# Layer 0 of a two-layer graph network: one-hot numbers read from PSUM, and GpSimd's gathers without waits for the one-hot rows

## What is computed

```python
h = jnp.maximum(_layernorm(x), 0.0)
msgs = h[src]                                            # layer 0
summed = segment_sum(msgs, dst, num_segments=num_dst)
h_neigh = summed / jnp.maximum(deg, 1.0)[:, None]
x = x + relu(h @ W_self + h_neigh @ W_neigh + b)
h = jnp.maximum(_layernorm(x), 0.0)
xs = h[src]                                              # layer 1
e = sigmoid(relu(concat([xs, h[dst]]) @ We1 + be1) @ We2 + be2)
m = e * xs
m_sum, m_max = segment_sum(m, dst), segment_max(m, dst)
x = x + relu(concat([m_max, m_sum, h]) @ Wn1 + bn1) @ Wn2 + bn2
```

## Time and profile before

| | us |
|---|---|
| median of 3 runs (5727.77 to 5729.11) | 5728.72 |
| span of the profiled execution | 5726.5 |
| GpSimd busy | 4144.7 (72%) |
| VectorE busy | 4244.9 (74%) |
| TensorE busy | 3700.0 (65%) |
| ScalarE busy | 1898.2 (33%) |

### The profile page before, as it was taken

The page is one execution under the profiler, slowest core; times in us unless marked ns, Lnnn a source line. Parts: engine busy times, 40 slices in busy tenths (PEclk is TensorE's granted clock), DMA queues, the critical chain, the costliest instruction groups (busy, mean ns, idle before and its releaser), DMA issues.

```text
span 5726.5 us, 110353 instructions
## 1 busy us (share of the span) xinstructions
PE 3700.0 (65%) x25175; PEld 3357.9 (59%) x25176; DVE 4244.9 (74%) x9019; ACT 1898.2 (33%) x4035; POOL 4144.7 (72%) x3884
## 2 busy tenths in 40 slices
PE   0001888988888888545566666666666667767771
PEld 0001878888888888545555555556555666666660
DVE  5788778877777777467777777777787778888881
ACT  6101777877777777401111111111111111111110
POOL 5243666888888888777777777777777777777766
PEclk9999999999999999855555555555555555555555
DMA  7210112434344443443333333333444434444440
GB/s 233 77 36 14 25 40 66 122 122 125 121 124 125 124 125 123 139 107 104 106 111 107 113 111 113 111 113 111 119 113 117 119 112 124 117 119 126 123 114 22
DMA packets 402218, 611.87 MB, mean 107 GB/s; under 512 B 191933, under 2 KB 274979, under 8 KB 402107
## 3 DMA queue, kind: packets, MB, share of 16 engines
q0 software_dynamic: 182688, 377.75, 24.2%
q1 hardware_dynamic: 150357, 130.12, 7.1%
q10 hardware_dynamic: 69094, 103.21, 5.9%
HBM read 470.99 MB, written 118.43 MB: 103 GB/s over the span
## 4 chain that ended last, share of the span: by engine, by line
POOL 45%; issue 21%; PE 12%; DVE 11%; DMA 3%; DVEq 2%; ACTq 2%; ACT 2%; POOLq 1%; SPq 0%; PEld 0%
POOL counts_f L572 23%; POOL extra_f L572 16%; PE ps_acc L1785 5%; POOL records L594 2%; PE ps_acc L1884 2%; DVE msg L1443 1%; POOL own_rows L618 1%; PE ps_acc L1815 1%; DMA counts_f<-hA_table,stage 1%; DVE act_w L1432 1%; PE ps L1807 1%; DVE chunk_max L1448 1%; POOL out_dram L717 1%; DVE pre L1037 1%; DVE hot L1270 1%
## 5 line engine op out<-in xcount | busy, mean ns | idle before, releaser
L572 POOL DMA_INDIRECT counts_f<-hA_table,stage x2496 | 2368.2, 949 | 783.4 <-issue 751.2
L1785 PE MATMUL ps_acc<-msg,ident 128*128 128x64 f32 (+1 forms) x4974 | 1229.8, 427 | 1013.6 <-DVE msg L1443 1013.6
L1785 PEld LDWEIGHTS ps_acc<-msg,ident 128*128 128x128 f32 x4974 | 1115.4, 328 | 1119.5 <-DVE msg L1443 1117.8
L1601 ACT ACTIVATE counts_f<-ps 128x784 bf16<-128x784 f32 x1568 | 1267.8, 823 | 427.2 <-PE ps L1807 363.8
L572 POOL DMA_INDIRECT extra_f<-hA_table,estage x780 | 1085.1, 1391 | 237.7 <-issue 232.3
L1815 PE MATMUL ps_acc<-pieces_f,counts_f 128*128 128x192 bf16 x9604 | 1035.1, 249 | 1.8 <-ACT counts_f L1601 1.2
L1807 PE MATMUL ps<-hot 128*128 128x196 bf16 x6272 | 829.8, 256 | 226.5 <-ACT counts_f L1601 153.6
L1693 ACT ACTIVATE ps<-z,be_col 128x4 f32<-128x4 f32 x854 | 228.2, 267 | 2214.4 <-DVE z L1438 1954.8
L1426 DVE TENSOR_TENSOR pre<-counts_f,ps 128x512 f32 (+1 forms) x854 | 585.4, 685 | 482.5 <-SPq L864 310.0
L1815 PEld LDWEIGHTS ps_acc<-pieces_f,counts_f 128*128 128x128 bf16 x9604 | 897.0, 139 | 3.3 <-issue 2.1
L1807 PEld LDWEIGHTS ps<-hot 128*128 128x128 bf16 x6272 | 545.0, 99 | 318.3 <-issue 292.3
(11 more groups left out here) (244 smaller groups left out, 3228.1 us busy)
## 6 DMA issues: line engine op xcount, KB each, us to landing
early_rows<-extra_f SPq DMA_DIRECT2D x196, 384.0 KB
counts_f<-early_rows ACTq DMA_DIRECT2D x98, 768.0 KB
counts_f<-hA_table,stage POOLq DMA_INDIRECT x2496
counts_f<-counts_f SPq DMA_DIRECT2D x78, 288.0 KB, 2.6
own<-own_rows ACTq DMA_DIRECT2D x98, 128.0 KB, 2.2
extra_f<-hA_table,estage POOLq DMA_INDIRECT x780
hA_table<-node ACTq DMA_DIRECT2D x98, 96.0 KB
sorted_rows<-srt SPq DMA_DIRECT2D x14, 252.0 KB, 2.6
```

The lines of the kernel that those rows point to most:

```text
L572: return pool.indirect_dma_start(to, None, table, bass.IndirectOffsetOnAxis(ap=idx, axis=axis))
L1601: act.activation(counts[:, c, nodes, :].rearrange("p (b h) t -> p b (h t)", h=2), ps_pairs[g & 1][:, :].rearrange("p (b w) -> p b w", b=BA ...
L1785: return pe.matmul(ps_sum[:, 0:D], ident[:, :], rows, start=False, stop=False, skip_group_check=True)
```

## The change

The numbers stay in PSUM. `load_edges` loads the lists of two tiles so that partition a holds nodes 2a and 2a + 1 side by side. Partitions 0 to 63 are then one tile and 64 to 127 the next, and `edge_ids` copies 128 columns once. A transpose of 64 partitions now gives even nodes on partitions 0 to 63 and odd ones on 64 to 127 at once. `edge_values` and `val` are gone; the one-hot instruction reads `ps_val` in `ps_t`. As that buffer is single, the transposes of the next tile's numbers wait until this tile's one-hots are all made (`s_hot`), and stand before the pairs of group 12. VectorE's first one-hots of a phase wait for them (`s_tr`). `edge_ids` moves to the second phase of a pair. The other transposes move from `ps_t` to `ps_y`; for that `cat_transpose` stands after group 7, `cat_copy` after eviction 8 and `product` after group 9. GpSimd's `spread` waits are removed.

```diff
-        idx_lo = sb("idx_lo", [P, 2, 2, RUN], BF16)
-        idx_hi = sb("idx_hi", [P, 2, 2, RUN], BF16)
-        val = sb("val", [P, 2, 2, PAIRS], BF16)
+        idx_lo = sb("idx_lo", [P, 2 * RUN], BF16)
+        idx_hi = sb("idx_hi", [P, 2 * RUN], BF16)
...
-        ps_idx = ps_t[:, 0:P].bitcast(BF16)
+        ps_val = ps_t[:, 0:PAIRS].bitcast(BF16).rearrange("p (w n) -> p w n", w=2)
+        ps_T = ps_y[:, 0:P]
+        ps_new = ps_y[:, P:P + D]
+        ps_ab = ps_y[:, BANK // 2:BANK]
...
-                        if spread and n % half == half // 2:
-                            wait_alone(pool, s_hot, jj * (8 * SUBS) + (c * (4 * SUBS) + (2 + n // half) * (2 * SUBS) + 6))
...
-            def load_edges(t, c):
-                sp.dma_start(win[:, c, :], sorted_rows[bass.ds(t * P, P), 0:RUN]).then_inc(s_win[c], 16)
+            rows_by_two = sorted_rows.rearrange("(a h) w -> a h w", h=2)
+            def load_edges(q):
+                sp.dma_start(win[:, :, :], rows_by_two[bass.ds(q * P, P), :, 0:RUN]).then_inc(s_win, 16)
...
-                v.tensor_copy(idx_lo[:, :, :, :], twice(src_lo[:, :])).then_inc(s_prep, 1)
-                v.tensor_copy(idx_hi[:, :, :, :], twice(src_hi[:, :])).then_inc(s_prep, 1)
+                v.tensor_copy(idx_lo[:, :], src_lo[:, :]).then_inc(s_prep, 1)
+                v.tensor_copy(idx_hi[:, :], src_hi[:, :]).then_inc(s_prep, 1)
...
-                    wait_alone(v, s_val, q * 4 + (2 * c + 2))
+                    wait_alone(v, s_tr, q * 2 + (c + 1))
...
-                    ids = val[:, c, which, s * SUB_PAIRS:(s + 1) * SUB_PAIRS].rearrange("p (b e) -> p b e", e=2)
+                    ids = ps_val[:, which, s * SUB_PAIRS:(s + 1) * SUB_PAIRS].rearrange("p (b e) -> p b e", e=2)
...
-                if ids and c == 0:
+                if ids and c == 1:
                     edge_ids(q + 1)
...
-            def edge_values(q, k):
...
-                    act.activation(val[half, k & 1, :, :], by_parity[half, :, :, h], ACT.Copy).then_inc(s_val, 1)
...
-                    if g == 4 and ids:
-                        edge_values(q, c + 1)
...
-                    if g == 7 and mean:
+                    if g == 8 and mean:
                         cat_copy(q - 1, c)
...
+                half = slice((k & 1) * PAIRS, ((k & 1) + 1) * PAIRS)
...
-                    last = pe.transpose(ps_idx[:, w * P:(w + 1) * P],
-                                        ids[:, k & 1, :, :].rearrange("p h k -> p (h k)"), ident_b[:, :])
+                    last = pe.transpose(ps_val[:, w, :], ids[half, :], ident_b[half, half])
...
+                    if g == 12 and ids:
+                        wait_alone(pe, s_hot, q * (4 * SUBS) + (c + 1) * (2 * SUBS))
+                        edge_transposes(q, c + 1)
...
-                    if g == 4 and ids:
-                        edge_transposes(q, c + 1)
-                    if g == 6 and mean:
-                        if ids:
-                            wait_alone(pe, s_val, q * 4 + (2 * c + 4))
+                    if g == 7 and mean:
                         cat_transpose(q - 1, c)
-                    if g == 8 and mean:
+                    if g == 9 and mean:
                         product(q - 1, c)
```

More of the change, by code:

```diff
@@ L425, in gnn_kernel @@
         s_xadd = sem("s_xadd")
-        s_win = [sem(f"s_win{c}") for c in range(2)]
+        s_win = sem("s_win")
         s_prep = sem("s_prep")
         s_tr = sem("s_tr")
-        s_val = sem("s_val")
         s_hot = sem("s_hot")
@@ L684, in _ @@
                     early_gather(jj, c, READY[1])
-            early_gather(TPAIRS // 2, 0, READY[1], spread=False)
+            early_gather(TPAIRS // 2, 0, READY[1])
             early_rest(GROUPS_L0)
@@ L785, in next_tiles @@
                     wait_alone(sp, s_prep, q * 2 + 2)
-                    for c in range(2):
-                        load_edges(q * 2 + (c + 2), c)
+                    load_edges(q + 1)
                 wait_alone(sp, s_x1, q * 2 - 2)
@@ L792, in _ @@
                 sp.wait_ge(s_srtw[h], 16 * TITER)
-            for t in range(2):
-                load_edges(t, t)
+            load_edges(0)
             sp.wait_ge(s_h0w, H0_DMAS)
@@ L798, in _ @@
             sp.wait_ge(s_prep, 2)
-            for t in range(2, 4):
-                load_edges(t, t & 1)
+            load_edges(1)
             sp.wait_ge(s_prep, 4)
-            for t in range(4, 6):
-                load_edges(t, t & 1)
+            load_edges(2)
             for q in range(2, 5):
@@ L1245, in edge_ids @@
             def edge_ids(q):
-                for c in range(2):
-                    v.wait_ge(s_win[c], q * 16 + 16)
-                ids = win[:, :, :].rearrange("p c k -> p (c k)")
+                v.wait_ge(s_win, q * 16 + 16)
+                ids = win[:, :, :].rearrange("p h k -> p (h k)")
                 st.done(v.tensor_single_scalar(src_lo[:, :], ids, P - 1, ALU.bitwise_and))
@@ L1288, in new_x @@
                 wait_alone(v, s_y, q * 2 + (c + 1))
-                v.scalar_tensor_tensor(out=node[:, c, H:H + D], in0=ps_y[:, 0:D], scalar=0.0, in1=xh[:, c, 0:D],
+                v.scalar_tensor_tensor(out=node[:, c, H:H + D], in0=ps_new, scalar=0.0, in1=xh[:, c, 0:D],
                                        op0=ALU.max, op1=ALU.add).then_inc(s_x1, 1)
@@ L1620, in cat_copy @@
                 wait_alone(act, s_catT, q * 2 + (c + 1))
-                act.activation(catT[:, :], ps_t[:, P:2 * P], ACT.Copy).then_inc(s_catTs, 1)
+                act.activation(catT[:, :], ps_T, ACT.Copy).then_inc(s_catTs, 1)
             def root(q, c):
@@ L1625, in root, with phase @@
                 act.activation(std[:, :], mv[:, 1:2], ACT.Sqrt, bias=eps_col[:, 0:1]).then_inc(s_std1, 1)
-            def phase(q, c, new=True, ids=True, mean=True, last=True):
+            def phase(q, c, new=True, mean=True, last=True):
                 for g in range(PAIR_GROUPS):
@@ L1641, in phase @@
                         root(q - 1, c)
-            edge_values(0, 0)
             phase(0, 0, mean=False, last=False)
@@ L1654, in _ @@
             phase(q, 0)
-            phase(q, 1, ids=False)
-            phase(q + 1, 0, new=False, ids=False)
-            phase(q + 1, 1, new=False, ids=False)
-            phase(q + 2, 0, new=False, ids=False, mean=False)
+            phase(q, 1)
+            phase(q + 1, 0, new=False)
+            phase(q + 1, 1, new=False)
+            phase(q + 2, 0, new=False, mean=False)
             own_by_tile = own_rows.rearrange("(p t) w -> p t w", p=P)
```

31 lines of the change are left out of this document (11 added, 20 removed).

## The result

The changed kernel takes **5570.76 us** (median of 4 runs, 5569.31 to 5571.78) where the kernel before took 5728.56 beside it (5727.77 to 5729.11). The ratio is 0.9724, with a 95% interval of 0.971 to 0.9737: 2.8% faster. The prediction was 5568. The profiled spans are 5726.5 before and 5570.0 after.

What follows compares the result with a forecast made beforehand. GpSimd, its gathers held by VectorE's one-hots, was taken to bound layer 0 from 1182 us. Terms of -15, -5, -4, -120 and -17 us sum to -161 on a 5726.5 span: 5568 us median, range 5540 to 5650.

Steps and rivals of the forecast that it cites:

- GpSimd was the bound: Layer 0 from 1182 us: gathers wait for VectorE's one-hots; with numbers in PSUM, 1.41 us each becomes 0.95.
- VectorE's pace on PSUM: One-hot instructions reading numbers from PSUM: forecast to keep 1.23 and 1.78 us.
- the other answer: Rival: one-hots run at the single rate from PSUM, 2.30 and 3.44 us; about 6490 us in all, chance 0.16.
- ScalarE's copies: Two val copies between evictions 4 and 5 go, so eviction 6 and pairs 8 come earlier: net -0.44 us per phase.
- the 17.31 that the sum started from: Phase length in us at 1008, taken as the pace of TensorE with ScalarE once GpSimd is off the path.
- The hand-over: VectorE's first one-hot of a phase waits about 0.8 us later for transposes; 0.4 us of slack, priced at 0.
- the rival of 5600 to 5650: Slack before one-hots missing, or product in group 9 waits for its copy: phases 0.5 to 1.0 us longer; chance 0.10.
- Late edges: Stretch 751 to 1008 us, where VectorE is full and keeps its work: -5 us (+5 to -10).
- The ends: Layer 0's start, 593 to 751: -15 us from faster records and scatter; its end: -17 us without GpSimd's backlog.
- the -161 that I had summed: Total of all terms in us, on a span of 5726.5: -15 - 5 - 4 - 120 - 17.

Runs made afterwards that it cites:

- the spare copies: The changed kernel with two unread ScalarE copies of 64 x 128 bf16 per phase added behind eviction 4; ratio 0.9796.
- the moved store: The changed kernel with ScalarE's issue of the table-store DMA behind eviction 9 instead of between evictions 5 and 6; 5529.03 us, ratio 0.9655.

## Why the prediction was right, and where it was off

**GpSimd was the bound, and the second SBUF operand held it: right, and shown.** The gathers went from 1.41 to 0.95 us, and the operand's place alone makes the difference of 120 us.

**VectorE's pace on PSUM: right.** This was the open question, with 0.16 on the other answer. The one-hots took 1223 and 1781 ns, 6 and 3 ns less than from SBUF. The argument from the earlier trace rows, that the width and not the place sets the rate, held. The Trainium skill's page "VectorE: DVE Perf Modes", section "The perf-mode tier table", gives the single rate for any PSUM operand in a tensor_tensor; this trace disagrees for a two-byte operand from PSUM beside one from SBUF.

**ScalarE's copies: right in size.** -0.44 per phase was in the sum, and the spare copies gave 0.41 back. The phase came out at 16.96 instead of 16.87, 0.35 below the 17.31 that the sum started from. The working has 0.55 for the copies, where its own rows give 0.61 (1088.84 to 1089.45), and doesn't say why.

**The hand-over: priced at 0, and that held, but for a wrong reason.** The slack wasn't 0.4 but some 0.05 us, since I counted one hand-over where there are two. Had the product or the one-hots been a little longer, the rival of 5600 to 5650 would have come. I should have put more than 0.10 on it. That rival has a slip as well: from 18.81 to 17.4 are 1.4 us per phase and not 1.2, and its 5600 goes by 1.4.

**Late edges: no gain where I had -5.** The +1.6 itself is not clear of the scatter: the same 14 phases take 256.3 us in the changed kernel with GpSimd's waits put back, and 258.2 in the kernel before without them. The first eleven take 200.6 before and 201.4 after, with VectorE busy about 170 of 201 in both. What it gained by not meeting own_rows it doesn't show; why not wasn't tried.

**The ends: right.** -12.9 for -15 and -17.4 for -17. How near the first is, is partly chance, as the first 8 phases take 158.1 us in the kernel before and 165.0 in the same kernel without the spread waits, which only come later. The last early gather starts at 2274.07 and ends 60.4 us behind the last mark, without a backlog.

**A part of the hit was luck.** My own terms came to -147, 14 us short of the -161 that I had summed. Two differences outside the sum, -3.6 before the first mark and -6.1 in layer 1, filled most of that. Neither can be put down to the change. In ten traces layer 1's gathers have a mean of either 946 or 949 ns, with 3293 to 3295 or 3301 to 3302 us for the layer: 946 in the kernel before without the spread waits and 949 in the one with the moved store. The first mark lies anywhere from 588.6 to 596.6 in kernels whose work up to there is nearly the same.

## What to carry over

When GpSimd's indirect DMAs are slow, look what VectorE runs over them: a tensor_tensor with both inputs in SBUF holds each one that starts behind it until it has ended, and here moving one input to PSUM freed GpSimd without a cost at VectorE for two-byte data. When a value goes from one engine to another and back, count a hand-over at each crossing, 0.33 and 0.39 us here, and test a slack by moving the step one place later. After a bound has gone, read the next engine's small waits: one DMA issue that stood between two evictions was worth another 0.7%.

## What the runs showed of the hardware that I had not expected

A bf16 tensor_tensor with one operand from PSUM ran as fast as with both from SBUF, or 3 to 6 ns faster (1223 to 1229, 1781 to 1784 ns). TensorE's clock fell to 1.2 GHz behind two waits of 1.70 and 0.76 us, in some phases and not in others with waits of 1.69 and 0.76. A gather that is held ends a fixed 0.82 us after the instruction that holds it, whether that lasts 1.2 or 3.4 us, and one that starts within the first 0.04 us of it isn't held. And in a set of runs the kernel before was 38% longer, and TensorE, ScalarE and VectorE of three other kernels stopped for 5 to 12 us in each phase while GpSimd went on; a ratio to the kernel before, taken beside it, doesn't mend that, since the two kernels were stretched by different amounts.
